# Down product of the experts with the split activations stationary, its sum with tokens on partitions

## The reference

```python
x = x + _L0_attn_ref(_layernorm(x), Wq, Wk, Wv, Wo, gamma, beta)
def body(acc, ws):                 # over the 32 experts
    guw, dw, w_e = ws
    gu = x @ guw.T
    g, u = jnp.split(gu, 2, axis=-1)
    y = u * jax.nn.silu(g) @ dw.T
    return (acc + y * w_e[:, None], None)
out, _ = jax.lax.scan(body, init, (gate_up_w, down_w, comb.T))
x = x + out                        # on the normalised x above
```

## Time and profile before

| | |
|---|---|
| median of 3 runs | 1826.33 us (1824.3 to 1828.45) |
| the profiled execution | 1824.45 us |
| its span, first to last instruction | 1822.7 us |
| mean granted TensorE clock | 0.989 |
| PE busy | 1723.3 us (95%), 17993 matmuls |
| DVE, ACT, POOL busy | 1475.5, 1446.1, 1407.8 us |

### The profile page before, as it was taken

One profiled execution on the slowest core, in us unless ns is written; L12 is line 12 of the kernel. 1 busy time (PEld: TensorE's weight loads), 2 busy tenths in 40 slices (PEclk: granted clock), 3 DMA queues, 4 the chain that ended last, 5 costly groups with the idle time before them and its releaser, 6 DMA issues.

```text
span 1822.7 us, 50405 instructions
## 1 busy us (share of the span) xinstructions
PE 1723.3 (95%) x17993; PEld 1016.7 (56%) x17993; DVE 1475.5 (81%) x4485; ACT 1446.1 (79%) x2396; POOL 1407.8 (77%) x1177
## 2 busy tenths in 40 slices
PE   5788999999999999999999999999999999998967
PEld 1455556565555656555565655556565555555642
DVE  8887878888787888888788888878888888787547
ACT  3778778887878888787887878888787888877854
POOL 2356797878879787887878788787888978688964
PEclk9899999999999999999999999999999999999989
DMA  6252443435354352634434264343436444253303
GB/s 205 50 123 65 107 118 95 123 78 141 94 124 103 95 126 66 152 94 114 111 90 125 71 153 99 102 123 86 121 78 152 101 101 106 63 132 83 90 30 100
DMA packets 180812, 191.02 MB, mean 105 GB/s; under 512 B 22482, under 2 KB 146258, under 8 KB 180434
## 3 DMA queue, kind: packets, MB, share of 16 engines
q1 hardware_dynamic: 180564, 187.80, 41.1%
HBM read 81.28 MB, written 5.24 MB: 47 GB/s over the span
## 4 chain that ended last, share of the span: by engine, by line
PE 63%; POOL 15%; issue 7%; ACT 7%; DVE 6%; DMA 2%; SPq 1%; ACTq 0%; POOLq 0%; DVEq 0%
PE bank_s L361 13%; PE bank_r L361 13%; PE bank_v L361 13%; PE bank_g L361 7%; PE bank_u L361 7%; PE bank_x L361 6%; POOL p_lo L1440 6%; POOL a_lo L1459 4%; POOL expert_room L1455 4%; PE bank_v L370 3%; ACT p L805 1%; ACT p_hi L743 1%; ACT bank_x L759 1%; DVE max_junk L1079 1%; ACT v_hi L743 1%
## 5 line engine op out<-in xcount | busy, mean ns | idle before, releaser
L1440 POOL TENSOR_TENSOR p_lo<-p,p_hi 128x1280 f16<-128x1280 f32 x256 | 671.2, 2623 | 204.7 <-ACT p_hi L743 204.5
L805 ACT ACTIVATE p<-bank_s,back 128x512 f32<-128x512 f32 (+1 forms) x768 | 457.4, 613 | 74.5 <-POOL p_lo L1440 37.2
L1079 DVE CUSTOM_DVE_ANT_0 max_junk<-bank_r,mask 128x512 f16<-128x512 f32 (+2 forms) x960 | 427.4, 485 | 72.3 <-PE bank_r L361 67.4
L361 PE MATMUL bank_s<-score_ops 128*128 128x512 f16 (+3 forms) x2048 | 410.8, 302 | 5.5 <-ACT p L805 5.1
L743 ACT ACTIVATE p_hi<-p 128x1280 f16<-128x1280 f32 x256 | 324.4, 1267 | 21.1 <-PE bank_v L361 18.9
L1455 POOL TENSOR_TENSOR expert_room<-expert_room 128x512 f32<-128x512 f32 x240 | 304.5, 1275 | 38.6 <-DVE expert_room L1177 25.7
L1459 POOL TENSOR_TENSOR a_lo<-expert_room,a_hi 128x512 f16<-128x512 f32 x240 | 277.5, 1162 | 13.8 <-ACT a_hi L743 13.7
L361 PE MATMUL bank_v<-v_hi,p_hi 128*128 128x65 f16 x2530 | 257.0, 195 | 5.9 <-DVE oT L1097 3.0
L361 PE MATMUL bank_v<-v_lo,p_hi 128*128 128x64 f16 x2530 | 256.6, 193 | 0.0
L361 PE MATMUL bank_v<-v_hi,p_lo 128*128 128x65 f16 x2530 | 256.3, 194 | 0.0
L361 PEld LDWEIGHTS bank_v<-v_hi,p_hi 128*128 128x128 f16 x2530 | 232.2, 98 | 36.2 <-DVE oT L1097 10.2
(11 more groups left out here) (212 smaller groups left out, 3553.5 us busy)
## 6 DMA issues: line engine op xcount, KB each, us to landing
score_ops<-nat SPq DMA_DIRECT2D x768, 128.0 KB, 2.5
expert_room<-comb_rows SPq DMA_DIRECT2D x480, 128.0 KB, 2.9
xt<-in_x SPq DMA_DIRECT2D x16, 256.0 KB, 3.0
xb<-in_x SPq DMA_DIRECT2D x16, 256.0 KB, 2.9
out_y<-expert_room SPq DMA_DIRECT2D x16, 256.0 KB, 2.6
score_ops<-comb_rows SPq DMA_DIRECT2D x32, 128.0 KB, 3.0
expert_room<-in_gate_up SPq DMA_DIRECT2D x1, 2048.0 KB, 10.7
score_ops<-rowmaxT SPq DMA_DIRECT2D x128, 4.0 KB
```

The lines of the kernel that those rows point to most:

```text
L361: return pe.matmul(dst, lhsT, rhs, start=start, stop=stop, skip_group_check=shared)
L805: act.activation(p32[:, h % P_SLOTS, at:at + cols], bank[score_bank(h, u)][:, 0:cols], ACT.Exp, scale=back[:, SC_SCORE:SC_SCORE + 1]).then ...
L1079: done = dve.tensor_tensor_reduce(max_junk[:, k % 2, at:at + cols], bank[b][:, at:at + cols], mask[:, S - cols:S], 1.0, NEG, ALU.add, ALU. ...
L1440: pool.tensor_tensor(p_lo[:, slot, :], p32[:, slot, :], p_hi[:, slot, :], ALU.subtract).then_inc(p_lo_done, 1)
```

## The change

`down_product` swaps its operands: for each block of 128 tokens the split activations are stationary and the 128 x 128 weights move, three matmuls of 128 columns for each of four blocks, twelve in place of three of 512 columns. The sum of the batch lies in bank x with tokens on partitions. The bank's accumulation is opened by the first matmul of the first block of pair 0 alone and closed by the last of pair 15. `copy_out` and `turn_out` go, with their two semaphores; `add_experts` waits for the last down product and reads bank x directly; bank x is held until it has. Nothing else changes in any order.

```diff
             def down_product(m, j):
                 if j == 0:
-                    take(XB, yT_done, m + 1)
+                    take(XB, out_ready, m + 1)
                 if m == 0 and j == 0:
                     pe.wait_ge(w_lo_done, PARTS)
                 pe.wait_ge(a_lo_done, m * EP + j + 1)
-                product(bank[XB][:, :], wh(WD, j * D, D), wl(WD, j * D, D), a_hi[:, j % 2, :], a_lo[:, j % 2, :],
-                        j == 0, j == EP - 1).then_inc(down_mm, 1)
-
-            def turn_out(m):
-                take(XB, out_ready, m + 1)
-                turn32(bank[XB], yT).then_inc(yT_turned, 1)
+                for c in range(C):
+                    rows = slice(c * P, c * P + P)
+                    done = product(bank[XB][:, rows], a_hi[:, j % 2, rows], a_lo[:, j % 2, rows], wh(WD, j * D, D), wl(WD, j * D, D),
+                                   j == 0 and c == 0, j == EP - 1 and c == C - 1, True)
+                done.then_inc(down_mm, 1)
...
-            def copy_out(m):
-                act.wait_ge(down_mm, (m + 1) * EP)
-                copy(late[:, :], bank[XB][:, :]).then_inc(yT_done, 1)
...
             def add_experts(p):
-                dve.wait_ge(yT_turned, p + 1)
+                dve.wait_ge(down_mm, (p + 1) * EP)
```

In the written-out orders each `turn_out(...)` is taken out of PE's and each `copy_out(...)` out of ACT's list:

```diff
-                down_product(n - 2, 15); times_v(n, 0, V); turn_out(n - 2); scores(n, 3, 0); max_scores(n, 7, 2, R0, R1)
+                down_product(n - 2, 15); times_v(n, 0, V); scores(n, 3, 0); max_scores(n, 7, 2, R0, R1); scores(n, 3, 1)
...
-            down_product(15, 14); down_product(15, 15); turn_out(15)
+            down_product(15, 14); down_product(15, 15)
```

More of the change, by code:

```diff
@@ L665, in _ @@
             down_product(12, 14); scores(14, 2, 2); max_scores(14, 7, 1, R0, R1); down_product(12, 15); scores(14, 3, 0)
[L666 to L679, removed]
+            max_scores(14, 7, 2, R0, R1); times_v(14, 1, V); scores(14, 3, 1); values(14, 4, R0); values(14, 5, R1)
@@ new lines, in _ @@
+            turn_maxima(14, 3, V); scores(14, 3, 2); scores(14, 4, 0); turn_heads(14, 0, V); scores(14, 4, 1)
+            times_v(14, 2, V); values(14, 6, R0); scores(14, 4, 2); values(14, 7, R1); turn_h2(13); scores(14, 5, 0)
+            times_v(14, 3, V); scores(14, 5, 1); turn_heads(14, 1, V); logit_product(13); gate_product(13, 0, G)
+            scores(14, 5, 2); times_wo(14, 0, V); up_product(13, 0, U); turn_h(15, V); gate_product(13, 1, G)
+            scores(14, 6, 0); project(15, 0, R0); scores(14, 6, 1); times_v(14, 4, V); project(15, 1, R1)
@@ new lines, in _ @@
+            gate_product(13, 2, G); scores(14, 6, 2); turn_weights(13); scores(14, 7, 0); max_scores(15, 0, 0, R0, R1)
+            scores(14, 7, 1); scores(14, 7, 2); gate_product(13, 3, G); times_v(14, 5, V); max_scores(15, 0, 1, R0, R1)
+            up_product(13, 1, U); scores(14, 8, 0); turn_heads(14, 2, V); scores(14, 8, 1); scores(14, 8, 2)
+            max_scores(15, 0, 2, R0, R1); up_product(13, 2, U); project(15, 2, R0); project(15, 3, R1); scores(14, 9, 0)
+            up_product(13, 3, U); gate_product(13, 4, G); max_scores(15, 1, 0, R0, R1); scores(14, 9, 1); scores(14, 9, 2)
@@ L680, in _ @@
+            times_v(14, 6, V); max_scores(15, 1, 1, R0, R1); scores(14, 10, 0); down_product(13, 0); gate_product(13, 5, G)
+            max_scores(15, 1, 2, R0, R1); down_product(13, 1); project(15, 4, R0); project(15, 5, R1); up_product(13, 4, U)
+            gate_product(13, 6, G); turn_maxima(15, 0, V); up_product(13, 5, U); scores(14, 10, 1)
             max_scores(15, 2, 0, R0, R1); times_v(14, 7, V); up_product(13, 6, U); max_scores(15, 2, 1, R0, R1)
@@ L700, in _ @@
             project(15, 14, R0); down_product(13, 13); scores(15, 2, 1); times_wo(14, 3, V); scores(15, 2, 2)
-            project(15, 15, R1); down_product(13, 14); down_product(13, 15); times_v(15, 0, V); turn_out(13); scores(15, 3, 0)
+            project(15, 15, R1); down_product(13, 14); down_product(13, 15); times_v(15, 0, V); scores(15, 3, 0)
             max_scores(15, 7, 0, R0, R1); max_scores(15, 7, 1, R0, R1); scores(15, 3, 1); scores(15, 3, 2); times_v(15, 1, V)
@@ L725, in _ @@
             times_v(15, 15, R0); turn_heads(15, 6, V); turn_heads(15, 7, R0); down_product(14, 12); down_product(14, 13)
-            times_wo(15, 3, V); down_product(14, 14); down_product(14, 15); turn_out(14); turn_h2(15); logit_product(15)
+            times_wo(15, 3, V); down_product(14, 14); down_product(14, 15); turn_h2(15); logit_product(15)
             up_product(15, 0, S1); gate_product(15, 0, R1); gate_product(15, 1, G); up_product(15, 1, U); turn_weights(15)
@@ L908, in _ @@
[L908 to L912, removed]
@@ L918, in _ @@
[L918 to L921 removed]
+                exps(n, 2, 0); exps(n, 2, 1); exps(n, 2, 2); p_high(n, 2); exps(n, 3, 0); residual_apply(n - 1); exps(n, 3, 1)
@@ new lines, in _ @@
+            p_high(15, 0); unit_high(13, 13); exps(15, 1, 1); exps(15, 1, 2); unit_high(13, 14); o_high(14, 7, V)
+            exps(15, 2, 0); exps(15, 2, 1); unit_high(13, 15); qk_high(15, 14, R0); p_high(15, 1); qk_high(15, 15, R1)
+            exps(15, 2, 2); p_high(15, 2); residual_apply(14); exps(15, 3, 0); exps(15, 3, 1); exps(15, 3, 2); p_high(15, 3)
+            exps(15, 4, 0); second_apply(14); h2_high(14); exps(15, 4, 1); v_high(15, 4, R0); copy_maxima(15, 3, V)
+            gate_tanh(14, 0, G); exps(15, 4, 2); o_high(15, 0, V); gate_tanh(14, 1, G); route(14); p_high(15, 4)
@@ L982, in _ @@
+            unit_high(15, 11); unit_high(15, 12); gate_tanh(15, 15, R1); unit_high(15, 13); unit_high(15, 14)
+            unit_high(15, 15)
         @block.vector
```

128 lines of the change are left out of this document (63 added, 65 removed).

## The result

| | before | after |
|---|---|---|
| median of 22 runs each | 1826.41 us (1823.99 to 1829.64) | 1828.88 us (1825.33 to 1834.0) |
| the profiled execution | 1824.45 us | 1831.94 us |
| ratio, 95% interval | | 1.0015 [1.0008, 1.0022] |

What follows compares the result with a forecast made beforehand. PE was busy 95% and held 63% of the chain, with ACT leading at the changed place. Loop periods -1.74, turn_out(12) +0.2, batches 0 and 14 +0.5, the end -1.3: total -2.3 us, 1824.0 us; range 1818.0 to 1829.5.

Steps and rivals of the forecast that it cites:

- 0.42 us gained per period at `residual_apply`: In the loop, removing ACT's copy and PE's transposes starts the apply earlier, gaining 0.42 us per period (bounds 0 and 0.60).
- The cost per down product: On PE, twelve matmuls of 128 columns take 0.673 us, 0.025 us more per down product.
- How many of them are on the path: Of a period's sixteen down products, eleven count on the path, costing 0.275 us per period (bounds 0 and 0.40).
- the wait that ends at 853.33: PE's wait for a_lo of POOL, said to hide the added cost of three down products per batch.
- The end: After the last down product, copy and transposes stand in a row with nothing beside them; removing them gains 1.3 us.
- `turn_out(12)`: At batch 12's turn the shift ends late, so only some 0.06 us can be won against 0.275: +0.2 us.
- The prediction's span of its own case: The times the forecast's own case was said to cover, 1822.7 to 1829.5 us.
- C: Residual normalisation sets its own time, the apply moves at most 0.1 us, all down products count: 1831.0 us; chance 0.12.
- B: PE's extra columns fall into its many small waits, so only the gains count: 1819.7 us; chance 0.36.
- D: Weight loads of fresh activations don't overlap on PE, so a down product takes 1.16 us: 1956 us; chance 0.02.
- the marks given for right and wrong: Profile signs: 0.67 us down product, no ACT idle for bank x, apply right after add_experts, 106.7 us periods, end 1.3 shorter.
- three signs of being wrong: The apply does not move, periods change by over 0.3 us, or a step of 128 columns takes over 60 ns.

Runs made afterwards that it cites:

- e2: The changed kernel with the old 512-column down product, copy and transposes still out, experts' sum left unturned; 1824.19 us, ratio 0.9991 to the kernel before.
- e3: The changed kernel with times_v(n, 0) moved ahead of the last down product in PE's loop; 1824.13 us, ratio 0.9989 to the kernel before.
- e8: The changed kernel with a third buffer for the high half of head 2's probabilities in the twelve loop iterations; 1823.93 us, ratio 0.9991 to the kernel before.
- e9: The kernel of e8 with the exchange of e3 on top; 1824.6 us, ratio 0.9992 to the kernel before.
- e1: The kernel before with each down product cut into four blocks of 128 tokens, weights stationary, copy and transposes kept; 1830.75 us, ratio 1.0024.
- e6: The kernel before with each down product cut into eight blocks of 64 tokens, weights stationary, copy and transposes kept; 1835.56 us, ratio 1.0058.

## Why the prediction was wrong

**The term that failed: 0.42 us gained per period at `residual_apply`.** The step was "Without copy and wait, ACT could start the exponentials of head 2 unit 2 about 1.16 us earlier". That is so, but the prediction then went straight on to the exponentials of head 3 and asked of them only for their scores. Between the two stands `p_high(n, 2)`, which the order quoted ahead of the prediction shows, and whose wait for `times_v(n, 0)` is in the code. That wait ends when it did before, 0.3 us after the last matmul of `times_v(7, 0)` starts. The prediction did write a bound of 0 "if another wait takes over in full", but named no such wait. Measured: nothing at the apply relative to `add_experts` (1.24 us after its start, 1.22 before), 0.04 us per period with copy and turn gone alone (e2). That 0.42 was right for a kernel without this wait is shown by e3 (0.45) and e8 (0.44). Twelve times 0.42 are 5.0 us.

**The cost per down product** was right: 0.67 us for twelve matmuls; with a digit more it is 0.0226 us each, where 0.025 were taken.

**How many of them are on the path** was wrong, eleven taken, about sixteen measured. Two causes. The last two of a batch were said to be "in the 0.42"; with no gain they count by themselves. Three were held to be hidden by the wait that ends at 853.33. That wait, 0.3 us for `a_lo`, was read from the period after 811.80, which is 107.54 us long; in a clean period of the same trace, PE's waits (above) do not contain it. The prediction took its cover from a disturbed period, though the earlier trace rows had both lengths side by side. The per-period account then closes: 16 x 0.0226 = 0.36 for the blocks, less 0.03 that `p_high` comes sooner with the copy out of ACT's queue (0.31 to 0.29 after `times_v`; 0.04 in e2), gives +0.33, as measured, and with the 0.44 of e8 it gives -0.11 against before, its 106.76.

**The end**: forecast -1.3 us. After, the last chain is:

```profile
1825.18 1.47 PE bank_x L360 x12
1826.65 0.02 issue
1826.67 0.75 DVE expert_room L1180
```

From the start of the last but one down product to `add_experts` are 2.61 us (1824.06 to 1826.67) where there were 4.12 (1815.03 to 1819.15): -1.5, right in kind and size. The split did cost nothing there: at the lower clock the last product's matmuls of 128 columns start every 107 ns, those of 512 every 427 ns before, four times as much. But from `residual_apply(15)` to `add_experts(15)` the gain is only 0.84 (57.00 to 56.16), and the other 0.67 is not in batch 15's down products, which the sum had forgotten: from the first of them to the last but one are 26.39 us before and 26.40 after. It lies ahead of them, and the granted clock shows it (columns as in the earlier trace rows):

```profile
1763.79:1777.44 13.65, 5.67 (x27) 2.55 (x28) 7.14 (x31) 3.24 (x7) 1.66 (x4) 0.50 0.02 5
1777.44:1814.99 37.55, 30.64 (x133) 11.48 (x131) 34.49 (x48) 20.38 (x32) 20.71 (x16) 1.00 0.35 114
```
```profile
1773.49:1787.14 13.65, 7.01 (x31) 3.21 (x32) 6.55 (x31) 3.24 (x7) 1.66 (x4) 0.50 0.00 0
1787.14:1824.69 37.55, 30.86 (x267) 17.55 (x265) 33.78 (x46) 20.39 (x32) 21.34 (x16) 1.00 0.37 115
```

The clock goes from 0.50 to 1.00 at 1777.44 before, 15.29 us after the start of `residual_apply(15)`, and at 1787.14 after, 16.63 us after it; PE runs its gate and up products there without a wait, and 1.34 us more of them at half the clock cost 0.67 us. In the other kernels that point lies 13.4 to 16.4 us after the apply, for kernels with the same lists too (13.4 in e9, 15.1 in e8), so the change is not shown to be its cause.

**`turn_out(12)`** was right in kind: little can be won there, since the shift comes late. After, the same apply stands behind it:

```profile
1569.82 1.61 ACT L757 ACTIVATE bank_x<-y,shift,rstd 128x128 f32<-128x128 f32 x4 [1.08 <-POOL shift L1409]
```

**The sum again**, from what was measured: twelve periods of +0.33 are +4.0, the end -0.8, together +3.2 us; the ratio says +2.7 (1.5 to 4.0). The prediction's span of its own case, 1822.7 to 1829.5, had no working: by its bounds, nothing gained and sixteen products on the path, its sum gives 12 x 0.40 + 0.2 + 0.5 - 1.3 = +4.2, 1830.5. Over the eleven whole loop periods, longer ones included, the two profiles give +3.1 (1177.76 to 1180.84). The small terms at the beginning and at batches 12 to 14 lie below what two profiles can tell: from `residual_apply(13)` to `residual_apply(14)`, where after, e3 and e8 have the same lists, they take 109.68, 108.66 and 109.61 us.

**The rivals.** C (1831.0 us) came nearest. Its condition, an apply that moves by less than 0.1 us while the down products' cost stays, is what happened; its mechanism, that the normalisation sets its own time, holds only at `turn_out(12)`. In the loop the shift was ready 0.7 us before the apply. B fell with the gain it rests on, and the cost was not hidden either: of the 0.36 us that e1 adds in a clean period 0.34 came through. D is out, by the 0.67 us; so is, for these shapes, the figure of the Trainium skill ("TensorE: Matmul & The Clock Gate", section "Back-to-back issue gap"), about 81 ns for 128 columns: a load and matmul of 128 columns with fresh activations stationary take 56 ns here.

Of the marks given for right and wrong, the down product (0.67 us) and the end held. ACT has no idle time for bank x ahead of head 2's last exponentials, but that was sure once the copy was gone; its idle time stands behind them. The others failed in the kernel after: `residual_apply(6)` comes 2.75 us after batch 5's last down product ends and not 2.3, 0.5 us and not at once after `add_experts`, and the period is 107.20 and not 106.7. e8 has 2.29 us, 0.04 us and 106.76. Two of the prediction's three signs of being wrong came: the apply did not move, and the periods changed by over 0.3 us (0.33).

## What to carry to other kernels

Before a removed step is credited to its engine, write down every instruction that stands behind it up to the one whose start is to move, with each one's own waits in the code: a wait that ends while the engine is busy leaves no idle time in the trace, and it is the first to take the gain. Take covers and waits from a period whose length is the usual one; a longer period shows waits that are not there in most. A gain that a first change doesn't bring may be one exchange of neighbours away: with `times_v(n, 0)` ahead of the last down product, or a third buffer for one head, the same change runs in 0.9989 [0.9980, 0.9998] and 0.9991 [0.9982, 1.0001] of the time before instead of 1.0015 [1.0008, 1.0022]. That is faster than the kernel after beyond the intervals, and hardly faster than the kernel before.

## What the runs showed of the hardware

Splitting a product's 512 moving columns into four blocks of 128 costs 0.0226 us per three-matmul product at the granted clock of 1.00, and into eight blocks of 64 costs 0.052, although nine or twenty-one more weight loads of 97 to 98 ns each are issued per product: they run under the matmuls, which start every 56 ns (128 columns) or 29 ns (64), whether the new stationary operand is the same weights (e1) or fresh activations (after), and the price is the same in both. Per added matmul it is 2.5 ns at either size (22.6 by 9, 52 by 21). Each added matmul came with one more load, so these runs don't tell which of the two has the 2.5 ns. At the granted clock of 0.50 there is no such price: 107 ns for 128 columns, 427 for 512. The Trainium skill, "TensorE: Matmul & The Clock Gate", section "Wait — 56ns, not 53.3ns?", gives just this size to the matmul, a fixed 2.5 ns or so beside its columns at the higher clock; these runs agree, and with the other section of the same page, cited above, they do not. A loop that leaves PE only 1.2 us of waits in 106.87 passed a change of 0.36 us on as 0.34 (e1), and one of 0.83 as 0.86 (e6).
